# Down projection by feature, without TensorE transposes, and normalising by a PSUM bank of inverse maxima

## The reference, cut to what matters

```python
gate = x @ W_gate.T + lora(x, A_gate, B_gate)      # lora(.) = 0.5 * (. @ A.T) @ B.T, by entry
up   = x @ W_up.T   + lora(x, A_up, B_up)
act  = silu(gate) * up                             # tokens x 1376
down = act @ W_down.T + lora(act, A_down, B_down)  # tokens x 512
m    = clip(max(abs(down), axis=-1), 1e-5)         # one maximum per token
out  = ((down / m) @ Q.T) * (m * weight_scale) + bias   # Q: 512 x 512, from {-1.5,-0.5,0.5,1.5}
return x + out
```

## Time and profile before

| | |
|---|---|
| median of 3 runs | 907.25 us |
| the profiled execution | 907.95 us, its span 906.1 us |
| TensorE (matmul) busy | 890.4 us, 98% |
| VectorE busy | 350.9 us, 39% |
| ScalarE busy | 259.2 us, 29% |
| GpSimd busy | 87.2 us, 10% |
| granted clock of TensorE | 0.997 of full speed |
| DMA | 45.38 MB, 50 GB/s |

### The profile page before, as it was taken

How to read it: one execution, slowest core, us unless ns; L and a number is a source line. 1 busy time by engine, 2 the same in 40 slices (tenths; PEclk the granted TensorE clock), 3 DMA queues, 4 the chain that set the end, 5 groups by cost and what they waited for, 6 DMA issues and landing times.

```text
span 906.1 us, 13800 instructions
## 1 busy us (share of the span) xinstructions
PE 890.4 (98%) x3991; PEld 720.2 (79%) x3991; DVE 350.9 (39%) x757; ACT 259.2 (29%) x448; POOL 87.2 (10%) x119
## 2 busy tenths in 40 slices
PE   6899999999999999999999999999999999999997
PEld 6788888888888887888888888788878888788885
DVE  4755264233442225422453224432245322552225
ACT  2533252122422124211242113421143111522112
POOL 1111003000030000310003100031001210100200
PEclk9999999999999999999999999999999999999999
DMA  5563110211112011120111102111111111201001
GB/s 144 166 192 109 39 56 22 51 30 33 47 35 59 21 45 45 31 62 12 50 48 38 47 12 57 52 38 35 27 45 52 43 33 30 56 24 34 24 14 47
DMA packets 44661, 45.38 MB, mean 50 GB/s; under 512 B 13168, under 2 KB 31088, under 8 KB 44608
## 3 DMA queue, kind: packets, MB, share of 16 engines
q1 hardware_dynamic: 42208, 41.52, 16.9%
q10 hardware_dynamic: 2176, 2.89, 1.1%
q0 software_dynamic: 224, 0.46, 0.2%
HBM read 36.44 MB, written 8.39 MB: 49 GB/s over the span
## 4 chain that ended last, share of the span: by engine, by line
PE 95%; DVE 1%; DMA 1%; ACT 0%; issue 0%; SPq 0%; ACTq 0%; DVEq 0%
PE pw_up L1771 26%; PE pw_gate L1771 24%; PE pw_down L1844 24%; PE ps_misc L1872 6%; PE pw_td L1833 5%; PE pw_down L1857 2%; PE pw_up L1813 2%; PE ps_misc L1771 2%; PE pw_gate L1813 2%; PE ps_misc L1864 1%; DMA rows<-w_gu 1%; DMA x_raw<-x_feat 0%; DVE wt_split L1375 0%; DMA plan_room<-places 0%; PE ps_misc L1813 0%
## 5 line engine op out<-in xcount | busy, mean ns | idle before, releaser
L1844 PE MATMUL pw_down<-wd,wact_split 128*128 128x512 f32 x960 | 232.5, 391 | 0.0
L1771 PE MATMUL pw_up<-wxs,wgu 128*128 128x512 f32 x948 | 229.4, 391 | 0.0
L1844 PEld LDWEIGHTS pw_down<-wd,wact_split 128*128 128x128 f32 x960 | 180.3, 188 | 44.5
L1771 PE MATMUL pw_gate<-wxs,wgu 128*128 128x512 f32 x864 | 212.8, 395 | 0.1
L1771 PEld LDWEIGHTS pw_up<-wxs,wgu 128*128 128x128 f32 x948 | 178.4, 188 | 38.6
L1771 PEld LDWEIGHTS pw_gate<-wxs,wgu 128*128 128x128 f32 x864 | 161.2, 189 | 33.6 <-issue 0.5
L1395 DVE TENSOR_TENSOR wact_full<-pw_up,wact_full 128x512 f32<-128x512 f32 (+1 forms) x87 | 60.0, 690 | 297.2 <-PE pw_up L1813 294.9
L1025 ACT ACTIVATE wact_full<-pw_gate 128x512 f32<-128x512 f32 (+1 forms) x80 | 47.7, 597 | 279.3 <-PE pw_gate L1813 279.3
L1037 ACT ACTIVATE wact_split<-wact_full 128x512 fp32r<-128x512 f32 x80 | 50.5, 631 | 69.7 <-DVE wact_full L1395 69.7
L1400 DVE TENSOR_TENSOR wact_split<-wact_full,wact_split 128x512 fp32r<-128x512 f32 x80 | 55.7, 697 | 26.3 <-ACT wact_split L1037 26.3
L815 POOL TENSOR_TENSOR rows<-rows,bias 128x512 f32<-128x512 f32 x28 | 35.8, 1288 | 222.3 <-DMA rows<-x_tok 221.1
(11 more groups left out here) (137 smaller groups left out, 678.2 us busy)
## 6 DMA issues: line engine op xcount, KB each, us to landing
out<-rows SPq DMA_DIRECT2D x121, 64.0 KB, 1.6
rows<-x_tok SPq DMA_DIRECT2D x112, 64.0 KB, 1.8
rows<-w_gu SPq DMA_DIRECT2D x8, 512.0 KB, 3.9
x_raw<-x_feat SPq DMA_DIRECT2D x60, 64.0 KB, 1.7
x_more<-x_feat SPq DMA_DIRECT2D x56, 64.0 KB, 1.8
wb_raw<-b_rows SPq DMA_DIRECT2D x32, 92.0 KB, 2.9
low_room<-b_rows SPq DMA_DIRECT2D x32, 80.0 KB, 2.5
rows<-w_down SPq DMA_DIRECT2D x9, 256.0 KB, 4.1
```

Source lines behind the costliest of these rows:

```text
L1771: last = nc.tensor.matmul(bank, w, wxs[:, xp, k, :], start=(n == 0 and k == 0), stop=False, skip_group_check=(f == 0))
L1844: last = nc.tensor.matmul(pw_down[:, s, :], wact(ap, f)[:, s * P:(s + 1) * P], wd[:, wp, f, :], start=(f == 1 and n == 0), stop=False)
```

## The change

The down projection of tiles 0 to 6 is computed with features on the partitions: `wd` is stationary, `wact` moves, and bank `k` of `pw_down` holds 128 features x 512 tokens. The transposes of these tiles go. The maximum over features now runs across partitions; VectorE makes it: a maximum over the four banks for all tokens at once (`max_of_chunks`), a transpose of 32x32 blocks, a maximum within each, small copies and maxima between the quarters of the partitions, the inverse, and a copy and a second transpose that put the inverse of each token's maximum on all partitions, into `ps_misc` (`max_of_tokens`). Then VectorE multiplies the four feature blocks by that bank (`normalise`). All of this stands behind chunk 0's product and chunk 1's split. The loop of TensorE covers tiles 1 to 6; tile 7 is written out, with the down projection by token and its end as before. The output is written over the residual in `wx_res`, so a residual block is loaded when the store of the output in its slot has landed.

```diff
         def wide_drain(tile, k):                                # ScalarE
+                if k == 0:
+                    act.wait_ge(dt_lo, WSUBS * tile)
+                act.wait_ge(blocks_done, KC * tile + k + 1)
+                nc.scalar.activation(feat[:, k, :], pw_down[:, k, :], ACT.Copy).then_inc(drained, 1)
+            def wide_dt_hi(tile, s):
+                act.wait_ge(norm_ready, KC * (tile + 1))
+                if s > 0:
+                    act.wait_ge(ffn_done, WSUBS * tile + s)
+                nc.scalar.activation(wdt_split[:, HI, :, :], feat[:, :, s * P:(s + 1) * P], ACT.Copy
+                                     ).then_inc(dt_hi, 1)
...
-                    if not first and 1 <= f <= WSUBS:
-                        wide_normalise(tile - 1, f - 1, wnorm)
...
+            def max_of_chunks(tile):                            # VectorE
+                dve.wait_ge(drained, KC * (tile + 1))
+                nc.vector.tensor_reduce(max_room, feat.rearrange("p k t -> p t k"), AX_X, ALU.max,
+                                        apply_absolute_value=True).then_inc(max_steps, 1)
+            def max_of_tokens(tile):
+                tt, copy = nc.vector.tensor_tensor, nc.vector.tensor_copy
+                step = MAX_STEPS * tile + 1
+                dve.wait_ge(max_steps, step)
+                nc.vector.transpose(turned_room, max_room).then_inc(max_steps, 1)
+                dve.wait_ge(max_steps, step + 1)
+                nc.vector.tensor_reduce(token_max, turned_room.rearrange("p (j c) -> p j c", c=SEQ), AX_X, ALU.max
+                                        ).then_inc(max_steps, 1)
+                dve.wait_ge(max_steps, step + 2)
+                copy(other_max[0:64, :], token_max[64:128, :])
+                copy(other_max[64:128, :], token_max[0:64, :]).then_inc(max_steps, 1)
+                dve.wait_ge(max_steps, step + 3)
+                tt(token_max, token_max, other_max, ALU.max).then_inc(max_steps, 1)
...
+                nc.vector.reciprocal(token_inv, token_max).then_inc(max_steps, 1)
+                by_quadrant = token_max.rearrange("p (s a) -> p a s", a=4)
+                for a in range(4):
+                    quadrant = slice(32 * a, 32 * (a + 1))
+                    tt(ascale[quadrant, :], by_quadrant[quadrant, a, :],
+                       wscale[quadrant, :].to_broadcast([32, WSUBS]), ALU.mult).then_inc(ffn_scaled, 1)
+                dve.wait_ge(max_steps, step + 8)
+                copy(max_room.rearrange("p (j c) -> p j c", c=SEQ),
+                     token_inv[:, :, None].to_broadcast([P, WENTRIES, SEQ])).then_inc(max_steps, 1)
+                dve.wait_ge(max_steps, step + 9)
+                nc.vector.transpose(ps_misc[:, :], max_room).then_inc(max_steps, 1)
+            def normalise(tile):
+                dve.wait_ge(max_steps, MAX_STEPS * (tile + 1))
+                for k in range(KC):
+                    nc.vector.tensor_tensor(feat[:, k, :], feat[:, k, :], ps_misc[:, :], ALU.mult
+                                            ).then_inc(norm_ready, 1)
...
+                    if not first and f == 0:
+                        max_of_chunks(tile - 1)
                     if f < FC - 1:
                         wide_act_lo(tile, f)
+                        if not first and f == 1:
+                            max_of_tokens(tile - 1)
+                            normalise(tile - 1)
                         wide_ad_split(tile, f + 1, first)
...
-                    if not first and f < WSUBS:
-                        wide_scales(tile - 1, f, wnorm)
...
             def wide_down(tile, f, first):                      # TensorE
...
+                for k in range(KC):
+                    for n, (ap, wp) in enumerate(PASSES):
+                        last = nc.tensor.matmul(pw_down[:, k, :], wd[:, wp, f, k * P:(k + 1) * P], wact(ap, f),
+                                                start=(f == 1 and n == 0), stop=False)
...
-                    if not first and f in (2, 4, 6, 8):
-                        if f == 2:
+                    if not first and f in (3, 5, 7, 9):
+                        if f == 3:
                             pe.wait_ge(silu_done, FC * tile + 2)
                         else:
                             pe.wait_ge(out_ready, WSUBS * (tile - 1) + f // 2 - 1)
-                        wide_transposes(tile - 1, f // 2 - 1, ps_misc[:, :])
-                    if not first and f in (3, 5, 7, 9):
                         wide_ffn(tile - 1, f // 2 - 1, ps_misc[:, :], wdt_split)
...
+                def outputs_of(tile, s, second_next=True):      # SyncE
                     store_wide(sp, tile, s)
+                    if second_next:
+                        sp.wait_ge(stored, 16 * SUB_ENTRIES * (WSUBS * tile + s + 1))
+                        ahead, block = (tile, s + 2) if s < 2 else (tile + 1, s - 2)
+                        wide_residual(ahead, block, wx_res[:, s % 2, :], wxres_in[s % 2])
```

More of the change, by code:

```diff
@@ L169, in build @@
             wact_split = sb("wact_split", [P, 2, 2, WIDE], F32R, stack=wide)
+            with ExitStack() as maxima_first:
+                max_rooms = sb("max_rooms", [P, 2, WIDE], stack=maxima_first)
             wdt_split = sb("wdt_split", [P, 2, KC, P], F32R, stack=wide)
@@ L180, in build @@
             wact_full = sb("wact_full", [P, 2, WIDE], stack=wide)
+            maxima = sb("maxima", [P, 64], stack=wide)
             pw_down = ps("pw_down", [P, WSUBS, 512], stack=wide)
@@ L717, in wide_program @@
                 for s in range(WSUBS):
-                    outputs_of(last - 1, s)
+                    outputs_of(last - 1, s, second_next=s < 2)
                 end_of(last)
@@ L1093, in wide_tile @@
                     if not first and f == 0:
-                        for s in range(WSUBS):
-                            wide_drain(tile - 1, s)
+                        for k in range(KC):
+                            wide_drain(tile - 1, k)
                     if f < FC - 1:
@@ L1840, in wide_down, with wide_first_down, down_by_token @@
                 elif f == 1:
-                    pe.wait_ge(drained, WSUBS * tile)
+                    pe.wait_ge(drained, KC * tile)
+                for k in range(KC):
+                    for n, (ap, wp) in enumerate(PASSES):
+                        last = nc.tensor.matmul(pw_down[:, k, :], wd[:, wp, f, k * P:(k + 1) * P], wact(ap, f),
+                                                start=(f == 1 and n == 0), stop=False)
+                last.then_inc(down_done, 1)
+            def wide_first_down(tile):
+                pe.wait_ge(bd_ready, tile + 1)
+                pe.wait_ge(td_ready, tile + 1)
+                for k in range(KC):
+                    for n, (ap, wp) in enumerate(PASSES):
+                        last = nc.tensor.matmul(pw_down[:, k, :], wd[:, wp, 0, k * P:(k + 1) * P],
+                                                wact_first[:, ap, :], start=False, stop=(n == 2))
+                    last.then_inc(blocks_done, 1)
+            def down_by_token(f):
+                if f == 1:
+                    pe.wait_ge(drained, KC * (WTILES - 1))
                 for s in range(WSUBS):
@@ L1859, in wide_first_down, with last_transposes @@
                     last.then_inc(blocks_done, 1)
-            def wide_transposes(tile, s, bank):
-                pe.wait_ge(norm_ready, WSUBS * tile + s + 1)
+            def last_transposes(s, bank):
+                pe.wait_ge(norm_ready, WSUBS * (WTILES - 1) + s + 1)
                 for k in range(KC):
@@ L1874, in wide_ffn, with wide_tile @@
                 last.then_inc(ffn_done, 1)
-            def wide_tile(tile, first):
+            def wide_tile(tile, first, by_token=False):
                 if first:
@@ L1912, in wide_tile @@
                     wide_lora_a_down(tile, f - 1)
-                    wide_down(tile, f - 1, first)
-                    if not first and f in (2, 4, 6, 8):
-                        if f == 2:
+                    if by_token:
+                        down_by_token(f - 1)
+                    else:
+                        wide_down(tile, f - 1, first)
+                    if not first and f in (3, 5, 7, 9):
+                        if f == 3:
                             pe.wait_ge(silu_done, FC * tile + 2)
```

154 lines of the change are left out of this document (79 added, 75 removed).

## The result

The changed kernel takes 898.39 us (median of five runs, 896.87 to 899.95), the kernel before 907.25 (five runs, 905.58 to 909.73). The ratio is 0.9915, with a 95% interval of 0.9900 to 0.9931: 6 to 9 us faster. I had predicted 895.3 within 893.5 to 904.0. The sign and the range held; about a quarter of the forecast gain of 12.0 us did not come.

A forecast was written before the change was run, and what follows sets the result against it. TensorE, busy 98% and never waiting in the loop, bounds the kernel. 907.95 - 12.6 (transposes) + 0.7 (waits) = 896.05 us profiled, 0.7 above the median of the runs, so 895.3 us, range 893.5 to 904.

The forecast's parts named there:

- the two questions that decide: How much shorter TensorE's list of instructions gets, and whether VectorE's new work then makes TensorE wait.
- The transposes, 12.6 us: On TensorE, 28 groups of four transposes go, at 0.45 us each from distances; upper bound 16.8 us by busy time.
- Down by feature at nothing: On TensorE, swapping the stationary operand leaves number and size of down matmuls, at 0.228 us each; no cost.
- The maximum over the banks, 2.28 us: On VectorE behind the fourth drain, 2,048 elements read with a step of 512, priced at 2.28 us.
- rivals 2 and 3: Strided maximum at half pace (2.14 us more, 908.7 us, chance 0.09) or a third (4.28 more, 923.7, chance 0.07).
- rival 1: VectorE's block longer through slow transposes or small steps, product of chunk 2 late; 897.5 to 904 us, chance 0.27.
- The loop tile of 108.0 us: Sign of being right: a loop tile takes 108.0 us instead of 109.8.
- the 9 us: Sign of being wrong: TensorE's waits add to more than 9 us.
- The rest of the block, 8.2 us: VectorE's new work from first transpose through the four products, including fourteen small steps at 2.94 us; 8.2 us together.
- The slack of 0.2 us: VectorE's spare time before TensorE wants the product of chunk 2 for up of chunk 3; 0.2 us.
- Waits, 0.7 us: TensorE's waits for the product of chunk 2, charged at 0.1 us a tile, 0.7 us.
- SyncE's residual loads, ScalarE, the written-out tile: Later residual loads are hidden, ScalarE's lost normalisings bring no gain, and tile 7 written out costs nothing.

The follow-up runs named there:

- e5: Changed kernel with the maxima made bank by bank behind each drain and GpSimd started later in every tile; 893.58 us, 0.9857 of before.
- e3: Kernel before, with each of the loop's 28 groups of four transposes done twice; 917.95 us, 1.0133 of before.
- e7: Changed kernel with the maximum reading four contiguous neighbours instead of one element of each bank; 892.96 us, 0.9855 of before.
- e4: Changed kernel with nine instructions added behind its last output to time reads alone, so a second profile of it; tiles 1 to 6 took 108.62 us each.
- e1: Changed kernel with the maximum over the four banks made bank by bank behind each drain; 895.40 us, 0.9891 of before.
- e6: Changed kernel, strided maximum kept, with GpSimd held back until chunk 2's product in the loop and the last tile; 898.33 us, 0.9905 of before.

## Why the prediction was right, and what in it was wrong

- **What bounds the kernel.** Right: TensorE without a wait, and the two questions that decide.
- **The transposes, 12.6 us.** Right in kind, a little small. With no wait left a tile takes 107.87 instead of 109.81 (e5), 1.94 us or 0.485 a group, and the whole stretch is 13.9 us shorter. Doubling them cost 0.42 a group (e3). My 0.45 from distances lies between; the busy time, 0.60 a group or 16.8 us, lies beyond both.
- **Down by feature at nothing.** Right: 12 loads in 2.69 to 2.72 us, as before.
- **The maximum over the banks, 2.28 us.** Wrong, and it is the step that failed. It measured 3.85. I had its cause as rivals 2 and 3, at half and at a third of the pace, that is 4.4 and 6.6 us. The factor was 1.6, so neither came out, and their sign, a second wait at up of chunk 2, did. The trace of before had only the contiguous rate. I took it for the sum and left all else to two chances, 0.09 and 0.07, with nothing between full pace and half.
- **That the range held is in part luck.** The time fell where rival 1 had it, 897.5 to 904, but for the cause of rivals 2 and 3: the transposes and small steps of rival 1 were not too long, and at half the pace, by my own reckoning, the time would have been 908.7, outside the range. The loop tile of 108.0 us that I had named as the sign of being right measured 108.6 to 109.9, and the waits, 9.2 us at the weight loads and 3.8 at the matmuls, stand at the edge of the 9 us that I had named as the sign of being wrong.
- **The rest of the block, 8.2 us.** Measured 7.7 to 7.8: the fourteen small steps took 2.6 instead of 2.9, the transposes 0.70 and 0.73, the products 0.62 each. The slack of 0.2 us would have been 0.75 (e5), enough.
- **Waits, 0.7 us.** They cost 7.4 us: 772.2 - 764.8. Of these 6.0 go with the contiguous read alone (e7), the meeting in tile 1 among them; the waits that e7 keeps, all in tile 1 and the last tile beside GpSimd, go with the remaining 1.4 us. In e4's execution the waits cost 1.4 us less.
- **GpSimd.** Not in my sum. I had checked that VectorE's idle time covered the new block, and not what else runs in that time: in tile 1 GpSimd starts 4.9 us ahead of product 2 and in the last tile earlier still, and there the two engines meet. In the other tiles it starts 0.1 to 1.0 us ahead, and the second wait is 0.67 to 0.82 us.
- **SyncE's residual loads, ScalarE, the written-out tile.** Right, no wait stands there.
- **The sum.** -13.9 + 7.4 = -6.5 us from tile 1 on, where I had -11.9. The medians moved by 8.9, with an interval of 6 to 9; the two executions of the changed kernel give 6.4 and 7.8 without the start, and what the start adds to the medians is not shown.

## What to carry to other kernels

When work is moved to an engine that is idle more than half of the time, follow its order from the instruction that frees it to the one that the bound engine waits for: here 0.75 us of slack was all there was, at 47% busy. Price each read by its step: on VectorE a maximum of 2,048 float32 took 2.29 us up to a step of 8 bytes and 3.6 to 3.8 from 16 bytes on, and 3.85 in the kernel. Seven passes over contiguous tiles took as long in all, but they can start behind the first drain, and it is the part behind the last drain that counts. And look at what GpSimd does in the time that you fill on VectorE.

## What the runs showed of the hardware that I had not expected

- VectorE's instructions with two SBUF operands, or a one-operand pass at the pace of two elements, took up to 3.3 times as long beside GpSimd's (1.40 us for 0.43, 1.66 for 0.69), and a small one 1.29 for 0.19. The small one ended 0.04 us behind GpSimd's, so it had waited for it. The four products whose second operand is the PSUM bank took 0.62 a piece in tile 1 too, with GpSimd working beside them. The Trainium skill, "SBUF — State Buffer", "Who interferes with whom", says that just these kinds contend with GpSimd, over a port that the two share; by that rule, the trace agrees.
- In the changed kernel the strided maximum ran beside GpSimd in the last tile at 3.88 us against 3.85: a reduction was not touched.
- A wait of TensorE of 2.38 us was followed, 1 us later, by 3 us at a granted clock of 0.50, the level of 1.2 GHz (e1), and one of 2.81 us by none (e6, granted clock 1.00 throughout and twelve loads in 2.61 us). What tells them apart stays open.
